# A mixture-of-experts and attention block: combine weights spread over the partitions by GpSimd's indirect transfers instead of SP's broadcasts

## The reference

```python
x = x + 0.5 * _L0_ffn_ref(_layernorm(x, axis=-1), L0_ffn_gate_weight, L0_ffn_gate_up_proj, L0_ffn_down_proj)
x = x + _L0_attn_ref(_layernorm(x, axis=-1), L0_attn_Wq, L0_attn_Wk, L0_attn_Wv, L0_attn_Wo)
x = x + 0.5 * _L0_ffn_ref(_layernorm(x, axis=-1), L0_ffn_gate_weight, L0_ffn_gate_up_proj, L0_ffn_down_proj)
```

```python
def body(acc, params):
    w_gu, w_d, ce = params
    gu = x @ w_gu.T
    g, u = jnp.split(gu, 2, axis=-1)
    h = jax.nn.silu(g) * u
    return (acc + h @ w_d.T * ce[:, None], None)
out, _ = jax.lax.scan(body, jnp.zeros_like(x), (gate_up_proj, down_proj, combine.T))
```

## Time and profile before

| | |
|---|---|
| median of 2 runs | 2420.05 us |
| the profiled execution | 2418.05 us |
| its span, first to last instruction | 2416.3 us |
| mean granted clock of PE | 0.997 |
| busy PE / PEld / DVE / ACT / POOL | 94 / 63 / 65 / 50 / 43% |
| moved by DMA | 80.24 MB, mean 33 GB/s |

### The profile page before, as it was taken

How to read it: one execution, slowest core, us unless ns; L and a number is a source line. 1 busy time by engine, 2 the same in 40 slices (tenths; PEclk the granted TensorE clock), 3 DMA queues, 4 the chain that set the end, 5 groups by cost and what they waited for, 6 DMA issues and landing times.

```text
span 2416.3 us, 48432 instructions
## 1 busy us (share of the span) xinstructions
PE 2280.5 (94%) x19616; PEld 1517.7 (63%) x19616; DVE 1577.1 (65%) x3099; ACT 1215.7 (50%) x1953; POOL 1044.5 (43%) x863
## 2 busy tenths in 40 slices
PE   0199999999999999999999999999999999999999
PEld 0188886555556556655555655555555655588887
DVE  6545556977777777777777777676776773345443
ACT  0123332156655656656666656666666665633332
POOL 0066664344343444344343433433433433366665
PEclk9999999999999999999999999999999999999999
DMA  5111112101110101111011011101101010011010
GB/s 191 54 36 29 34 37 58 29 14 31 31 30 19 48 21 37 31 25 41 11 37 37 18 33 28 32 3 39 31 21 30 13 29 19 11 37 28 19 37 19
DMA packets 96327, 80.24 MB, mean 33 GB/s; under 512 B 40292, under 2 KB 88676, under 8 KB 95720
## 3 DMA queue, kind: packets, MB, share of 16 engines
q1 hardware_dynamic: 95240, 76.09, 11.2%
q10 hardware_dynamic: 864, 1.05, 0.1%
HBM read 64.25 MB, written 12.85 MB: 32 GB/s over the span
## 4 chain that ended last, share of the span: by engine, by line
PE 90%; DVE 6%; DMA 2%; issue 1%; SPq 0%; POOL 0%; ACT 0%; ACTq 0%; POOLq 0%; DVEq 0%
PE PS L1015 41%; PE PS L1031 21%; PE PS L1043 11%; PE PS L1074 11%; PE PS L989 2%; DVE arena L854 1%; PE PS L1055 1%; PE PS L966 1%; PE PS L992 1%; PE PS L1113 1%; DMA ident<-ident_c 1%; PE PS L1099 1%; DVE WGU L694 1%; DVE amax L681 1%; PE PS L975 0%
## 5 line engine op out<-in xcount | busy, mean ns | idle before, releaser
L1015 PE MATMUL PS<-XT,WGU 128*128 128x256 f16 x9216 | 1117.6, 274 | 11.3 <-DVE arena L831 3.7
L1015 PEld LDWEIGHTS PS<-XT,WGU 128*128 128x128 f16 x9216 | 875.0, 98 | 242.7 <-issue 132.2
L513 POOL TENSOR_TENSOR arena<-arena 128x512 f16<-128x512 f32 x384 | 444.6, 1158 | 1199.8 <-ACT arena L585 1199.8
L854 DVE TENSOR_REDUCE arena<-PS 128x1 f32<-128x512 f32 x1024 | 658.2, 685 | 370.0 <-PE PS L1043 368.0
L608 ACT ACTIVATE arena<-PS,fac 128x512 f32<-128x512 f32 x1024 | 646.3, 684 | 235.8 <-PE PS L1055 234.5
L578 ACT ACTIVATE arena<-PS,fac 128x512 f32<-128x512 f32 x384 | 263.9, 687 | 763.0 <-PE PS L1015 763.0
L1031 PE MATMUL PS<-WD,arena 128*128 128x256 f16 x4608 | 569.4, 274 | 6.5 <-POOL arena L513 6.3
L1031 PEld LDWEIGHTS PS<-WD,arena 128*128 128x128 f16 x4608 | 432.4, 98 | 146.8 <-issue 89.5
L508 POOL TENSOR_TENSOR arena<-arena 128x512 f32<-128x512 f32 x384 | 487.3, 1269 | 49.3 <-DVE arena L839 27.7
L831 DVE SCALAR_TENSOR_TENSOR arena<-arena,PS 128x512 f32<-128x512 f32 x384 | 261.4, 681 | 295.9 <-ACT arena L578 295.4
L1043 PE MATMUL PS<-arena 48*128 48x512 f16 x1024 | 312.2, 382 | 7.2 <-DMA arena<-k_scratch 4.5
(11 more groups left out here) (111 smaller groups left out, 842.6 us busy)
## 6 DMA issues: line engine op xcount, KB each, us to landing
arena<-ce_scratch SPq DMA_DIRECT2D x256, 128.0 KB, 3.2
arena<-wgu SPq DMA_DIRECT2D x2, 3072.0 KB, 14.9
arena<-q_scratch SPq DMA_DIRECT2D x96, 64.0 KB, 2.2
X<-x SPq DMA_DIRECT2D x1, 4096.0 KB, 31.2
arena<-ktab_c SPq DMA_DIRECT2D x16, 256.0 KB, 4.2
q_scratch<-arena SPq DMA_DIRECT2D x32, 128.0 KB, 1.7
out<-X SPq DMA_DIRECT2D x8, 512.0 KB, 3.0
arena<-wd SPq DMA_DIRECT2D x1, 3072.0 KB, 10.0
```

Of the source, the lines that this page charges most:

```text
L513: pool.tensor_tensor(hs[1][:, d % HS, :], tw[d % 2], hs[0][:, d % HS, :], ALU.subtract).then_inc(lo_done, 1)
L854: dve.tensor_reduce(mx[:, half * REP * QT + c:half * REP * QT + c + 1], PS[:, B_MAX + half, :], AX_X, ALU.max).then_inc(max_taken, 1)
L1015: ins = pe.matmul(PS[:, b, j * HALF_G:(j + 1) * HALF_G], WGU[w][:, kt, part * CHUNKS + c + j, :], XT[r][:, k % 2, kt, half * HALF_G:(half ...
```

## The change

The broadcasts leave SP. POOL issues four indirect transfers for each spread instead: each brings one row of 256 weights to each of 128 partitions, and the number of the row for each partition comes from a small table `cidx` (128 x 16 integers, a constant input, loaded once on ACT's queue). An indirect transfer reads from the start of a tensor, so `ce_scratch` becomes 16 tensors, one for each group. In POOL's loop the spread stands between `low(d)` and `weigh(d+1)`, at s = 2, 8 and 14 as before; that for the next group stands at s = 22, where SP had it at s = 21. `write_combine` stays on SP. The buffer `comb` is dropped and its values are put over `ld`.

```diff
--- before.py
+++ after.py
@@ -163,7 +163,7 @@
     return 2 * g + 2
 
 
-def build(nc, x, wgu, wd, wg, wq, wk, wv, wo, ident_c, ktab_c, kneg_c, out):
+def build(nc, x, wgu, wd, wg, wq, wk, wv, wo, ident_c, ktab_c, kneg_c, cidx_c, out):
     with ExitStack() as ctx:
         def sb(name, shape, dt=F32):
             return ctx.enter_context(nc.sbuf_tensor(name, shape, dt))
@@ -196,6 +196,7 @@
         rstd = sb("rstd", [P, GT])
         mhalf = sb("mhalf", [P, GT])
         pad = sb("pad", [P, 1])
+        cidx = sb("cidx", [P, 4 * 4], I32)
 
         lmax = sb("lmax", [P, GT])
         ld = sb("ld", [P, GT, EXPERTS])
@@ -208,7 +209,7 @@
         carry = sb("carry", [P, GT, TOPK])
         keep = sb("keep", [P, GT, TOPK])
         rw = sb("rw", [P, GT, TOPK])
-        comb = sb("comb", [P, GT, EXPERTS])
+        comb = ld
         combT = sb("combT", [P, GT, EXPERTS])
 
         amax = sb("amax", [P, N_SCALES])
@@ -262,7 +263,7 @@
         k_d = nc.dram_tensor("k_scratch", (2, BATCH, K_ROWS, SEQ), F16, kind="Internal").ap()
         v_d = nc.dram_tensor("v_scratch", (BATCH, KV, P, QT, 32), F32, kind="Internal").ap()
         m_d = nc.dram_tensor("m_scratch", (UNITS, 2, REP * QT, P), F16, kind="Internal").ap()
-        ce_d = nc.dram_tensor("ce_scratch", (PREPS, EXPERTS, GROUP), F32, kind="Internal").ap()
+        ce_d = [nc.dram_tensor(f"ce_scratch{k}", (EXPERTS, GROUP), F32, kind="Internal").ap() for k in range(PREPS)]
 
         PS = ctx.enter_context(nc.psum_tensor("PS", [P, 8, 512], F32))
 
@@ -272,7 +273,7 @@
 
 
         gu_in, small_in, x_in, d_in = sem("gu_in"), sem("small_in"), sem("x_in"), sem("d_in")
-        const_in, consts_set = sem("const_in"), sem("consts_set")
+        const_in, consts_set, cidx_in = sem("const_in"), sem("consts_set"), sem("cidx_in")
         amax_gu, amax_all, wmax_all = sem("amax_gu"), sem("amax_all"), sem("wmax_all")
         amax_d, wmax_d = sem("amax_d"), sem("wmax_d")
         scales_set, gu_split, d_split, small_split = sem("scales_set"), sem("gu_split"), sem("d_split"), sem("small_split")
@@ -354,19 +355,9 @@
 
                 sp.wait_ge(comb_ready, k + 1)
                 for pb in range(4):
-                    sp.dma_start(ce_d[k, :, :].rearrange("e (i q x) -> q e i x", i=GT, q=4)[pb],
+                    sp.dma_start(ce_d[k].rearrange("e (i q x) -> q e i x", i=GT, q=4)[pb],
                                  combT[32 * pb:32 * pb + 32, :, :]).then_inc(ce_out, 16)
                 sp.wait_ge(ce_out, 64 * (k + 1))
-
-            def spread(hh):
-
-                k, at, buf = hh // 4, hh // 2 % 2 * HALF_G, hh % 2
-                if hh >= 2:
-                    sp.wait_ge(w_done, 6 * (hh - 1))
-                for q in range(4):
-                    src = ce_d[k, :, at:at + HALF_G].rearrange("(s q) n -> q s n", q=4)[q, 4 * buf:4 * buf + 4, :]
-                    sp.dma_start(CB[32 * q:32 * q + 32, buf, :, :],
-                                 src.unsqueeze(0).to_broadcast([32, 4, HALF_G])).then_inc(cb_in[buf], 16)
 
             def tables(g):
 
@@ -438,14 +429,10 @@
                              X[:, g * GT:(g + 1) * GT, :]).then_inc(stored, 16)
 
             write_combine(0)
-            spread(0)
             for d in range(-1, SLOTS + 3):
                 k, s = divmod(d, PER_GROUP)
-                if d % 6 == 2 and (d + 4) % PER_GROUP and d + 4 < SLOTS:
-                    spread((d + 4) // 6)
                 if s == 21 and k + 1 < PREPS:
                     write_combine(k + 1)
-                    spread(4 * (k + 1))
                 if 1 <= k <= GROUPS:
                     if s == 1:
                         tables(k - 1)
@@ -521,14 +508,32 @@
                 pool.wait_ge(o_hi, v + 1)
                 pool.tensor_tensor(osp[1], otok_f, osp[0], ALU.subtract).then_inc(o_lo, 1)
 
+
+            def spread(hh):
+
+                buf = hh % 2
+                pool.wait_ge(ce_out, 64 * (hh // 4 + 1))
+                if hh >= 2:
+                    pool.wait_ge(w_done, 6 * (hh - 1))
+                for i in range(4):
+                    pool.indirect_dma_start(CB[:, buf, i, :], None, ce_d[hh // 4].rearrange("e (h n) -> (e h) n", h=2),
+                                            bass.IndirectOffsetOnAxis(ap=cidx[:, 4 * (hh % 4) + i:4 * (hh % 4) + i + 1], axis=0))\
+                        .then_inc(cb_in[buf], 16)
+
             inverse_roots(0)
             rows_low(0)
+            pool.wait_ge(cidx_in, 16)
+            spread(0)
             for d in range(-1, SLOTS + 2):
                 k, s = divmod(d, PER_GROUP)
                 if 0 <= d < SLOTS:
                     low(d)
                 if 1 <= k <= GROUPS and s in (10, 12, 14):
                     rope_low(k - 1, s // 2 - 5)
+                if d % 6 == 2 and (d + 4) % PER_GROUP and d + 4 < SLOTS:
+                    spread((d + 4) // 6)
+                if s == 22 and k + 1 < PREPS:
+                    spread(4 * (k + 1))
                 if d + 1 < SLOTS:
                     weigh(d + 1)
                 if 1 <= k <= GROUPS:
@@ -552,6 +557,7 @@
             for v, src in ((st_g, wg), (st_q, wq), (st_k, wk), (st_v, wv), (st_o, wo)):
                 act.dma_start(v, src).then_inc(small_in, 16)
             act.dma_start(ident[:, :], ident_c).then_inc(const_in, 16)
+            act.dma_start(cidx[:, :], cidx_c).then_inc(cidx_in, 16)
 
             def rows_high(i):
 
@@ -1222,7 +1228,10 @@
 
 
 def constants():
-    return {"ident_c": np.eye(P, dtype=np.float16),
+    hh, i, p = np.ogrid[0:4, 0:4, 0:P]
+    rows = (16 * (hh % 2) + 4 * i + p // 32) * 2 + hh // 2 % 2
+    return {"cidx_c": np.ascontiguousarray(rows.reshape(-1, P).T.astype(np.int32)),
+            "ident_c": np.eye(P, dtype=np.float16),
             "ktab_c": rope_tables(), "kneg_c": np.full((2, QKV * SEQ), -M_UNIT, np.float16)}
```

## The result

The changed kernel takes 2467.7 us (median of 2 runs, 2467.0 to 2468.5) against 2420.05 before: a ratio of 1.0198, 95% interval 1.0174 to 1.0223, so 2% slower, 48 us. That it is slower is clear; whether by more than the 2% that the prediction took as its bound is not, since the interval lies on both sides. The prediction had 2455, within 2418 to 2560. Its profiled execution took 2467.03 us, with a span of 2465.2.

The account below looks back on a forecast made before the run. PE was taken to bound the kernel, so only POOL's lateness beyond its slack counts: 27.5 + 2.2 + 2 + 3.4 = 35 us on the 2420.05 median, 2455 us, 1.5% slower, range 2418 to 2560.

Parts of the forecast that it names:

- What bounds the kernel, and where POOL may be late: PE bounds, with hardly any slack in the last two stages; a dense slot lets POOL be 3.46 us late.
- What is removed is worth nothing: Taking 256 transfers and their waits off SP's queue, and the other edits, were each put at nothing.
- The rival in which SP's free queue gains: Faster SP removes PE's 4.5 us wait for keys and the lower clock behind it: 6 us, 2414; chance 0.03.
- The price of an issue: POOL held 1.27 us per indirect issue, a fixed cost plus a loop over 128 items; four in a row 5.08 us.
- The two sentences of the Trainium skill: Small descriptor cost, dispatch about 0.05 us, four some 0.2 us; or about 1 us emission, four 4 us, loss 12 us.
- The sum: All places where POOL's four issues delay PE, added: 35 us, giving 2455 us, 1.5% slower.
- the start: PE's wait for the first `low`, behind the first spread, where issue isn't hidden: 4 x (1.27 - 0.43) = 3.4 us.
- 17 tight places: Spreads in dense slots, 8 in the first stage and 9 in the last: 5.08 - 3.46 = 1.62 us each, 27.5 us.
- the three that look like the earlier trace: Three slots at the end of attention with 4.34 us to spare: 0.74 us each, 2.2 us.
- the three in lengthened slots: Three first-stage slots lengthened by projections or attention's start: nothing, counting only beyond about 6 us.
- the 40 in attention: Spreads in the attention stage, 5.6 us to spare in the slot read; 2 us allowed for all 40.
- The dear branch: Issue price from 1.43 us: ACT late in attention too, loss 160c - 224 joins 84c - 71.5; 2551 at 1.75 us; chance 0.39.

Follow-up runs that it names:

- three fillers: Kernel before, with POOL doing three tiny 128x4 instructions in a row at 63 spread places, all transfers left on SP: 2419.9 us, ratio 1.0001.
- four (3.90 us): Kernel before, with POOL doing four tiny 128x4 instructions in a row at 63 spread places, transfers left on SP: 2433.4 us, ratio 1.0058.
- five (4.87): Kernel before, with POOL doing five tiny 128x4 instructions in a row at 63 spread places, transfers left on SP: 2456.3 us, ratio 1.0155.
- Experiment 1: Changed kernel with the spreads as SP's broadcasts again at SP's old places, other edits kept: 2419.46 us, ratio 1.0001.
- Experiment 4: Changed kernel with each indirect issue made twice, the second into a scratch tile, eight in a row: 2808.2 us, ratio 1.1609.
- experiment 7: Changed kernel with the first and next-group spreads back on SP, the other 48 indirect on POOL, one issue a turn: 2434.2 us, ratio 1.0060.

## Why the prediction was right, point by point

- **What bounds the kernel, and where POOL may be late.** Right. The slack of 3.46 us that the earlier trace rows gave by subtraction is well confirmed, 0.1 us too large for the hand-overs: three fillers (3.0 us) cost nothing, four (3.90 us) cost 0.55 at each plain dense place, five (4.87) cost 1.52, and in the changed kernel 4.95 us cost 1.61. Each leaves 3.34 or 3.35 us.
- **What is removed is worth nothing.** Right. Experiment 1 excludes a part of the other edits, and the wait for keys stayed at 4.8 us without the spreads in SP's queue. The rival in which SP's free queue gains is out.
- **The price of an issue.** 1.27 us was put down, and 1.25 us measured, but made of other parts: 0.95 us busy and 0.30 idle. My reason, a fixed cost and a loop over 128 rows, was wrong in the second half, since the rows are worth 0.04 us for 64. The figure came out by choosing the nearest row, which was luck as much as reasoning. So was the price of a place, 1.62 us for 1.61 found: POOL was held 4.95 us and not 5.08, and had 3.34 to spare and not 3.46, and the two errors cancel.
- **The two sentences of the Trainium skill** (DMA: Bandwidth & Descriptors). Its rule of a small cost for making descriptors, by which all would be hidden, is not what an indirect issue shows: 0.95 us of POOL each. Its other figure, about 1 us to the first byte, which the page puts down to the emission on GpSimd's cores, is close to that; the 0.30 us between two comes on top.
- **The sum** was 35 us and is 48, or 49 between the two profiled executions. The starts of every `down` in the two traces tell where it lies:

| | expected | found |
|---|---|---|
| the start | 3.4 | 3.5 |
| 17 tight places | 27.5 | 29.5 |
| the three that look like the earlier trace rows | 2.2 | 3.5 |
| the three in lengthened slots | 0 | 0.8 |
| dense turns without a spread | 0 | 6.5, in 7 turns |
| the 40 in attention | 2 | 5.2 |

The plain places cost 1.6 us each as expected, those at s = 14 1.8, and one 2.9. The term that was missing is that of the dense turns without a spread, which the prediction didn't count. At s = 12 PE waits three times for DVE's sum into X, because POOL's inverse root for the norm came late behind the spread at s = 8 (the row below). Once, at the end of attention, POOL's `outputs_split` makes `low` late a turn after the spread, for 1.7 us. Once the lower clock costs 1.7 us. Two turns at s = 5, 0.5 us each, are left unexplained. In attention most places cost nothing, as the earlier trace rows said, but one costs 1.6 us and three more 0.4 to 1.0. On the clock, I held a wait of 1.6 us to be far from lowering it, and none did; one wait of 2.7 us was enough, once.

```profile
184.85 1.48 PE L1037 MATMUL PS<-WD,arena 128*128 128x256 f16 x12 [0.53 <-DVE X L852]
```

- **What would show it.** PE's new wait for `low` in the dense stages: 33.5 us more, 23 places (about 30 us, 20 places expected). The wait at the start: 6.9 (8). Attention's length within a few us: 6. A clock of 1.00 throughout was wrong.
- **The dear branch.** Experiment 4 shows it: 389 us for 324 expected. PE's lower clock has 123 of them, and the waits, 266, are fewer than the formula had: in attention a place costs about 3 us without the clock, not 4.4.

## What to carry to other kernels

Before work goes onto an engine that looks half idle, take one slot of the timeline and subtract: from the end of each instruction to the start of the one that waits for it. That sum, here 3.46 us, and 3.35 by the runs, is what may be added in one place for nothing, and each us beyond it is paid in full, at each place. The busy share (43%) says nothing of it. And a single insertion under the limit isn't free if it comes in turns in a row: a turn with one took 4.33 us against a slot of 3.93, and the engine's other duties, here the norm, become late.

Here an indirect transfer costs POOL 1.25 us with 128 rows and 1.20 with 64, so cutting its rows gains next to nothing. Where the rows can be written as a plain pattern, a transfer from SP costs POOL nothing.

No version tried beats the kernel before. The nearest are the one that takes POOL's issues away (2419.5) and the one that keeps them plain (2424.1).

## What the runs showed of the hardware that I had not expected

- An indirect issue holds GpSimd for 0.95 us and is followed by 0.30 us of idle before the next; 64 rows in place of 128 save 0.04 us. A plain issue from the same engine takes 0.55 us and has no gap but for two of the 256.
- Twice (0.95 + 0.30) x 4 in a row, eight issues, make PE wait 6.4 us and bring its granted clock down to 0.57 over 8 us. After a wait of 2.7 us it fell once to 0.53 for 3.4 us; after waits of 1.45 to 1.63 it did not.
- Two of the 256 issues came after a long gap, 1.30 and 1.56 us in place of 0.30, with nothing in the profile that they waited for. They are the 114th and the 226th, 112 apart. In every run with 128 rows or with plain transfers it is the same two (with each issue twice also the 338th and the 450th; with 192 issues only the 114th), at gaps of 0.64 to 2.25 us; with 64 rows they are the 129th and the 253rd, at 2.5 us. So the gap comes with the count of issues and not with a time or a place in the kernel. Why is open.
- An issue of GpSimd can hold up a DVE instruction (experiment 7).
